# Layer 1's grouped experts: a counted loop written out tile by tile, with each tile's expert number loaded once and ahead

## The reference

```python
# layer 1, per token: gate over 9 experts, the two best, normalised
# expert e:  y = ( silu(x @ w1[e].T) * (x @ w3[e].T) ) @ w2[e].T
dim, hid, E, X = (128, 352, 8, 1)      # 8 + 1 experts, hidden width 352
TOP_K = 2
```

## Time and profile before

| | |
|---|---|
| median of 3 runs | 1991.06 us (1990.78 to 1992.78) |
| the profiled execution: its own time | 1985.47 us |
| its span, first to last instruction | 1983.8 us |
| PE busy over the span | 1555.5 us (78%), 12142 matmuls |
| DVE, ACT, POOL busy | 1341.1, 1044.5, 798.3 us |
| granted TensorE clock, mean | 0.905 of 2.4 GHz |

### The profile page before, as it was taken

One profiled execution on the slowest core, in us unless ns is written; L12 is line 12 of the kernel. 1 busy time (PEld: TensorE's weight loads), 2 busy tenths in 40 slices (PEclk: granted clock), 3 DMA queues, 4 the chain that ended last, 5 costly groups with the idle time before them and its releaser, 6 DMA issues. The chain is left out here.

```text
span 1983.8 us, 35609 instructions
## 1 busy us (share of the span) xinstructions
PE 1555.5 (78%) x12142; PEld 1065.2 (54%) x12143; DVE 1341.1 (68%) x2371; ACT 1044.5 (53%) x1857; POOL 798.3 (40%) x803
## 2 busy tenths in 40 slices
PE   5985887888865666636788889995489999869995
PEld 5753665665643444514566666663134444357884
DVE  7537777788799999585533337885873499556336
ACT  1458787787754545143433335663465477633441
POOL 1576555555698887257111113443320000006006
PEclk9997999999988888567899999997689999959998
DMA  4311111111000100456411113530652144021223
GB/s 146 99 62 52 52 38 46 51 34 46 17 26 25 31 23 10 161 186 159 70 44 44 42 44 68 89 62 20 175 88 51 33 67 66 5 90 54 87 79 85
DMA packets 153319, 130.35 MB, mean 66 GB/s; under 512 B 18929, under 2 KB 137864, under 8 KB 152914
## 3 DMA queue, kind: packets, MB, share of 16 engines
q1 hardware_dynamic: 140626, 104.57, 21.2%
q0 software_dynamic: 12544, 23.82, 4.6%
HBM read 77.08 MB, written 52.43 MB: 65 GB/s over the span
## 5 line engine op out<-in xcount | busy, mean ns | idle before, releaser
L667 POOL TENSOR_TENSOR xn_t<-xn_t,scan_du 128x512 f32<-128x512 f32 x256 | 321.6, 1270 | 179.9 <-ACT xn_t L809 100.0
L712 PE MATMUL banks<-scan_hc,ident 128*128 128x256 f32 x1024 | 294.9, 414 | 76.7 <-DVE scan_hc L864 76.7
L858 DVE TENSOR_TENSOR_SCAN xn_t<-banks,xn_t 128x512 f32<-128x512 f32 x256 | 311.3, 1216 | 42.0 <-ACT banks L799 35.7
L2287 ACT ACTIVATE att_pr<-banks 128x768 f32<-128x768 f32 (+1 forms) x256 | 234.2, 916 | 135.0 <-PE banks L2179 77.9
L799 ACT ACTIVATE banks<-delta,scan_exp_centre,a_neg 128x255 f32<-128x255 f32 x512 | 265.2, 559 | 49.9 <-DVE xn_t L858 49.4
L712 PEld LDWEIGHTS banks<-scan_hc,ident 128*128 128x128 f32 x1024 | 192.8, 207 | 139.6 <-DVE scan_hc L864 105.1
L864 DVE TENSOR_TENSOR scan_hc<-xn_t,banks 128x512 f32<-128x512 f32 x256 | 175.9, 687 | 26.8 <-PE banks L697 15.1
L918 POOL DMA_INDIRECT disp<-xn_tok,places x128 | 136.1, 1063 | 85.5 <-issue 61.3
L2332 DVE TENSOR_REDUCE att_mb<-banks 128x4 f32<-128x1024 f32 x128 | 153.9, 1221 | 22.9 <-PE banks L2146 18.1
L2195 PE MATMUL banks<-att_pr,att_vx 128*32 128x256 f32 (+1 forms) x2048 | 153.0, 372 | 5.0 <-ACT att_ot L2292 3.5
L2328 DVE TENSOR_REDUCE att_mb<-banks 128x6 f32<-128x768 f32 x128 | 121.5, 956 | 39.0 <-PE banks L2153 37.0
(11 more groups left out here) (360 smaller groups left out, 3340.0 us busy)
## 6 DMA issues: line engine op xcount, KB each, us to landing
scan_ew<-f_packed SPq DMA_DIRECT2D x12, 578.0 KB, 4.1
q_parts<-att_p_parts SPq DMA_DIRECT2D x16, 384.0 KB, 3.9
k_parts<-att_p_parts SPq DMA_DIRECT2D x16, 384.0 KB, 5.9
att_qs<-q_parts SPq DMA_DIRECT2D x64, 96.0 KB
att_ks<-k_parts SPq DMA_DIRECT2D x64, 96.0 KB
gau_ew<-f_packed SPq DMA_DIRECT2D x8, 578.0 KB
disp<-zeros SPq DMA_DIRECT2D x1, 4608.0 KB, 15.9
att_xin<-disp SPq DMA_DIRECT2D x72, 64.0 KB, 1.8
```

The source lines that it names most:

```text
L667: nc.gpsimd.tensor_tensor(bu[:, i % RING], b_sb[:, q % 2], du[:, b % 2, c:c + 1, :].to_broadcast([P, 2, T]), ALU.mult).then_inc(s.bu_made, 1)
L712: ins = nc.tensor.matmul(bank(Y_BANK)[:, c, :], g.ident[:], hc[:, i % RING, n, :], start=False, stop=(i % (PAIRS * DC) == PAIRS * DC - 1 a ...
L858: v.tensor_tensor_scan(rows(h[:, i % 2]), g.ps[:, DA + i % RING, :], rows(bu[:, i % RING]), 0.0, ALU.mult, ALU.add).then_inc(s.scan_done, 1)
L2287: nc.scalar.activation(pr[:, i % RING], g.ps[:, at:at + 2, 0:W], ACT.Exp, scale=scale).then_inc(s.p_ready, 1)
```

## The change

In `grouped`, the loop is gone: each engine's code is a Python `for` over all 72 tiles, so that every tile has instructions of its own, with DMA addresses and semaphore values as constants. Waits on values that are always reached are left out (first tiles), and so are the `sem_inc` that biased the counters. The order of the work on each engine is as before. On PE the expert number is loaded once a tile, into a register that `up` and, a tile later, `down` both use; the load stands behind `up(j+1)`, two tiles ahead. The matmuls still take the weights' address from a register.

```diff
-    def each(eng, body):
-        body(0, 0, 0, 0, 2)
-        body(1, 0, 1, 1, 2)
-        with eng.Fori(1, NJ // 2 - 1) as it:
-            for p in range(2):
-                body(it * 2 + p, it, p, 2, 2)
-        body(NJ - 2, NJ // 2 - 1, 0, 2, 1)
-        body(NJ - 1, NJ // 2 - 1, 1, 2, 0)
...
     def sync(sp):
         sp.wait_ge(r.scattered, 2 * NT * 16)
+        for j in range(NJ):
+            if j >= 2:
+                sp.wait_ge(s.turned, j - 1)
+            sp.dma_start(xin[:, j % 2, :], disp[j * P:(j + 1) * P, :]).then_inc(x_in[j % 2], 16)
...
-        def tile_expert(j):
-            return pe.value_load(r.tile_e[0:1, bass.ds(j, 1)], min_val=0, max_val=E1 - 1)
+        expert = {}
+        def load_expert(j):
+            if j < NJ:
+                expert[j] = pe.value_load(r.tile_e[0:1, j:j + 1], min_val=0, max_val=E1 - 1)
...
-        def up(j, p):
-            e = tile_expert(j)
+        def up(j):
             pe.wait_ge(s.xt_ready, j + 1)
...
-                                       rows(w13[:, bass.ds(e, 1), m * H1:(m + 1) * H1]), start=True, stop=True)
+                                       rows(w13[:, bass.ds(expert[j], 1), m * H1:(m + 1) * H1]), start=True, stop=True)
...
-        def down(j, p):
-            e = tile_expert(j)
...
+        load_expert(0)
+        load_expert(1)
+        transpose(0)
+        transpose(1)
+        up(0)
+        for j in range(NJ):
+            up(j + 1)
+            load_expert(j + 2)
+            transpose(j + 2)
+            turn_hidden(j)
+            down(j - 1)
+        down(NJ - 1)
```

More of the change, by code:

```diff
@@ L1223, in down @@
+        def down(j):
+            if j < 0:
+                return
+            p = j % 2
+            pe.wait_ge(s.ht_ready, j + 1)
+            if j >= 2:
+                pe.wait_ge(s.y_out, j - 1)
             for c, (lo, n) in enumerate(H1_CUTS):
                 ins = nc.tensor.matmul(g.ps[:, 4 * p, P:2 * P], ht[0:n, p, c, :],
-                                       rows(w2[0:n, bass.ds(e, 1), c * D:(c + 1) * D]),
-                                       start=(c == 0), stop=(c == len(H1_CUTS) - 1))
+                                       rows(w2[0:n, bass.ds(expert[j], 1), c * D:(c + 1) * D]),
+                                       start=(c == 0), stop=(c == NH - 1))
@@ L1227, in down @@
             ins.then_inc(s.y_ready, 1)
[L1229 to L1241, removed]
@@ L1252, in scalar, with silu @@
+        down(NJ - 1)
+        pe.wait_ge(s.y_out, NJ)
     def scalar(act):
         nc.scalar.preload_act_table(ACT.Silu)
-        act.sem_inc(s.ht_ready, 2)
-        def silu(j, p):
+        def silu(j):
+            if j >= NJ:
+                return
             act.wait_ge(s.ab_ready, j + 1)
[L1258 to L1263, removed]
+            if j >= 2:
+                act.wait_ge(s.h_ready, j - 1)
+            nc.scalar.activation(a[:, j % 2, :], g.ps[:, 4 * (j % 2) + 1, 0:H1], ACT.Silu).then_inc(s.a_ready, 1)
@@ L1264, in body @@
+        silu(0)
+        for j in range(NJ):
+            silu(j + 1)
             act.wait_ge(s.ht_turned, j + 1)
-            if before >= 2:
+            if j >= 2:
                 act.wait_ge(s.y_ready, j - 1)
-            n = H1_CUTS[-1][1]
+            p, n = j % 2, H1_CUTS[-1][1]
             nc.scalar.copy(ht[:, p, 0:2, :], g.ps[:, 4 * p + 3, 0:2 * P].rearrange("p (c t) -> p c t", c=2))
             nc.scalar.copy(ht[0:n, p, 2, :], g.ps[0:n, 4 * p + 3, 2 * P:3 * P]).then_inc(s.ht_ready, 1)
-        silu(0, 0)
@@ L1271, in scalar, with take @@
-        each(act, body)
     def vector(dve):
[L1274 to L1281, removed]
+        def take(j):
+            if j >= NJ:
+                return
+            dve.wait_ge(s.turned, j + 1)
+            nc.vector.tensor_copy(xt[:, j % 2, :], g.ps[:, 4 * (j % 2), 0:P]).then_inc(s.xt_ready, 1)
@@ L1289, in give @@
+        def give(j):
+            if j < 0:
+                return
+            p = j % 2
             dve.wait_ge(s.y_ready, j + 1)
-            if not isinstance(turn, int) or turn:
-                dve.wait_ge(stored[p], turn * 16)
+            if j >= 2:
+                dve.wait_ge(stored[p], j // 2 * 16)
             nc.vector.tensor_copy(yo[:, p, :], g.ps[:, 4 * p, P:2 * P]).then_inc(s.y_out, 1)
[L1294 to L1306, removed]
+        take(0)
+        take(1)
+        gated(0)
+        for j in range(NJ):
+            give(j - 2)
+            take(j + 2)
+            gated(j + 1)
+        give(NJ - 2)
+        give(NJ - 1)
     def gpsimd(pool):
-        def body(j, it, p, before, after):
-            pool.wait_ge(s.y_out, j + 3)
-            pool.dma_start(ybuf[bass.ds(j * P, P), :], yo[:, p, :]).then_inc(stored[p], 16)
@@ L1312, in gpsimd @@
-        each(pool, body)
+        for j in range(NJ):
+            pool.wait_ge(s.y_out, j + 1)
+            pool.dma_start(ybuf[j * P:(j + 1) * P, :], yo[:, j % 2, :]).then_inc(stored[j % 2], 16)
         for p in range(2):
-            pool.wait_ge(stored[p], NJ // 2 * 16)
+            pool.wait_ge(stored[p], len(range(p, NJ, 2)) * 16)
     job = Names()
```

53 lines of the change are left out of this document (28 added, 25 removed).

## The result

The changed kernel takes 1937.4 us (median of 4 runs, 1930.81 to 1939.94), the kernel before 1990.92 (4 runs beside them, 1989.99 to 1992.78). The ratio is 0.9732, with a 95% interval from 0.9713 to 0.975: 53.5 us faster. The forecast was 1940.5.

The account below looks back on a forecast made before the run. PE was taken to bound the stage, idle ahead of `up` while its sequencer loads a register and branches. Gains of 49.6 + 0.7 + 0.3 = 50.6 us from the 1991.06 us median gave 1940.5 us, range 1937 to 1957.

Parts of the forecast that it names:

- the two bounds: PE's period a tile without gaps: 2.29 us (gain 49.6 us) or 2.39 us (gain 42.8 us), from 3.02.
- the 0.10 us of the first matmul of `up`: First of `up`'s four matmuls takes 558 ns against 459; taken as the price of the pause before it.
- The margins of the moved load: Load between `up` and next transpose costs nothing: 0.3 us to spare at `xt`, 0.37 us at the transpose.
- Rival 1: A new wait at `xt` or the transpose takes part of the gain: 1961 us, or 1986 in full; chance 0.15.
- the second margin: Room at the transpose behind the moved load: 0.37 us, or about 0.2 if the load ends 0.3 us later.
- the wait at 1084.8: PE sequencer's wait ahead of `up`; its 51 ns, same as at L1235, read as not waiting for anything.
- The same load costs nothing elsewhere: Load ahead of `down` called free, since the sequencer was about 0.9 us ahead of its engine there.
- Hidden before, so worth nothing by itself: Removing each tile's second load, ahead of `down`, gains nothing itself but pays for the moved load.
- rival 2: Written-out code must be fetched, some 11 packets for PE: slower, 2001 us at 5.5 us a packet; chance 0.03.
- rivals 3 and 4: Denser PE granted a lower clock: 1958 us, chance 0.04; time given back behind the stage: 1990 us, chance 0.03.
- The head and the tail: Stage start: 0.3 us from loading the first expert number during PE's wait; last `up` and `down` gaps: 0.7 us.
- the sum: Whole gain: 49.6 us from tiles, 0.7 at the end, 0.3 at the head, 50.6 us; 1940.5 us from the median.

Follow-up runs that it names:

- e3: Changed kernel with a second register load and check right behind the first, its value unused: 2.451 us a tile, stage 189.5 us, median 2131.86 us.
- e10: Kernel before, with a third load, check and address a tile behind `up`, ahead of the transpose: 3.684 us a tile, ratio 1.0151 to 1.0238.
- e8: Changed kernel with its one load a tile moved to just ahead of `up`: 2.300 us a tile, stage 179.2 us, median 2110.59 us.
- e1: Changed kernel's straight code, but two loads a tile at their old places, ahead of `up` and `down`: 2.612 us a tile, stage 201.0 us, median 2142.76 us.
- e2: Loop kept, four tiles a turn on PE, one early load a tile into four registers, no bounds check: 2.293 us a tile, median 2126.34 us.
- e9: Kernel before without the bounds check of each load, loop and load places kept: 2.758 us a tile, stage 211.6 us, ratio 0.9841 to 0.9922.
- e11: Changed kernel with all SP input loads first and the attention's twelve loads held until after the stage: stage 171.6 us, median 2109.55 us.
- e4: Changed kernel unedited, run again on another chip: 2.292 us a tile, stage 179.2 us, median 2122.04 us, ratio 0.9747 to 0.9789.

## Why the prediction was right, point by point

**The bound, and the period of a tile.** Right. PE without gaps takes 2.292 us a tile, and of the two bounds 2.29 was the true one: the 0.10 us of the first matmul of `up` was the pause's. 68 x (3.019 - 2.292) is 49.4 where 49.6 was forecast.

**The margins of the moved load.** Right. `xt` was to be there 1.78 us behind `up`'s start, and the copy ends at 1.78 (1062.52 and 0.29, less 1061.03). The load lies beside `up`'s matmuls and PE waits for nothing. Rival 1 didn't occur. It isn't far off, though: a second load costs 0.16 us a tile (e3). Two steps of the working were unsound without harm. With a load 0.3 us longer the second margin would have been 0.07 us (3.47 - 3.4), not about 0.2. And the 51 ns of the wait at 1084.8 don't show that nothing was waited for: the row of L1210 above has 51 ns too, with half a microsecond of standing still behind it. What shows it is that the rows leave no gap: the check is over at 1084.65 and the instruction behind the wait starts at 1084.9.

**"The same load costs nothing elsewhere", and "Hidden before, so worth nothing by itself".** Wrong, and this is the step of the prediction that failed. I saw the sequencer 0.9 us ahead of its engine at the load ahead of `down` and took this lead for free time. But the sequencer of the kernel before never waited (no gap over 0.12 us). It had 3.02 us of instructions a tile against 2.29 us of PE's work. A lead that it had at one place was used up at the next, and a load at the hidden place made the next `up` later by as much: 0.665 us (e10). So the load ahead of `down` counted like the one ahead of `up`. In code written out it is enough that one of the two goes, whether the other stands ahead of `up` (e8: 2.300) or behind it (the changed kernel: 2.292). With the loop kept, no run takes away one load and nothing else. The gain came out right all the same, because it was computed from PE's floor and not from the loads: whatever brings the sequencer under 2.29 us gives 49 us, and what goes beyond gives nothing. That is luck as far as the reason goes: by the prediction an edit that only takes away the load ahead of `down` would have been costed at nothing, and from e1 to e8 that edit gave 21.7 us.

The runs put numbers on this budget. They have to be taken where the sequencer doesn't wait: 3.02 us in the kernel before, 2.45 in e3. So the loop's own instructions are 0.57 us a tile. Two loads of 0.665 us leave 2.45 - 1.33 = 1.12 us for all the rest of a tile in code written out, and with one load it needs 1.12 + 0.665 = 1.79 of 2.29 us. The 0.5 us left over is the half microsecond for which the changed kernel's sequencer is seen to stand still. e1 has the instructions of e3 and takes 0.16 us more: its loads stand behind the wait for `yo`, not ahead of it, and it waits there. So the place isn't always worth nothing. It can add a wait on top of the sum.

**The straight code is fetched; slower (rival 2).** Didn't occur, and neither did rivals 3 and 4. The granted clock is 1.00 in the stage, and the attention starts as much earlier as the stage is shorter. The page of the profile counts 100 instruction packets for the whole execution, where it counted 90 before (11 more were estimated), and PE has no idle time at all in the 100 us of the stretch.

**The head and the tail.** Both small. The 0.3 us of the first load came (from SP's issue to the first `up` 6.36 us instead of 6.65), but the first eight matmuls of `up` took 5.06 us instead of 4.34, and the head as a whole, the first step with it, lost 0.5 us. The tail gave 1.1 instead of 0.7. Together 49.4 - 0.5 + 1.1 is 50.0, as measured, where the sum had 50.6.

**The whole.** The range was 1937 to 1957, and 1937.4 lies at its lower edge, 3 us under the sum. The working had 2 us between runs, and the range went 3.5 us below the sum. The changed kernel's own runs spread over 9 us, which was the term I had made too small, and that the median still fell inside by 0.4 us is luck.

## What to carry to other kernels

Where PE's idle time is put down to an engine that had long been done, look whether its sequencer's rows follow one another without a gap, and add up what it does in a period: if that exceeds PE's work, each instruction costs its full length even where the sequencer is ahead, and the time falls until the sum is under PE's floor, and no further. So count register loads first (0.66 us each with the check), take away the easiest, and don't take a local lead of the sequencer for free room. The loop itself may stay where the sum allows it, as in e2. A wait for data can still come on top (e1, e9). To test whether a cost is hidden, double it.

## What was not expected of the hardware

- A register load with its check costs 0.665 us in sequence (e10), though its instruction lasts only 301 ns. The Trainium skill, "DMA: Bandwidth & Descriptors", section "Latency and other measured facts", gives such a load a floor of about 600 ns. The load itself is under that in every row here, 0.30 us at the median and 0.50 at the longest; the load with its check is near it.
- Short instructions take more room than their rows say. The loop left out was worth 0.57 us a tile to the sequencer (before less e3), while its branch, the longest instruction of it, lasts 0.208 us once in two tiles. The Trainium skill, "Perfetto Trace Analysis", section "Sequencer-only Instruction (DRAIN, etc)", says that the profile shows only the execution of such an instruction and leaves out the wait and the passing on of semaphores around it. The rows here agree: the wait at L1210 lasts 51 ns at 1062.3, the same as L1235 in the earlier trace rows, and the instruction behind it starts only at 1062.9, when the data is there.
- The matmuls at the head of the stage are slow even after a pause of 2.33 us: the first eight of `up` take 4.25 us (e11), where eight at full speed take about 2 x 1.45. The granted clock there is 1.00 from 1079.0 to 1083.4 us, with the pause in it and PE back at work since 1081.68, then 0.50 (1.2 GHz) to 1086.8, and 1.00 again. So the lower clock there isn't the 9 us wait's alone. What sets it stays open.
- The chips differ by 9% in the kernel before and in the changed one, and the changed one's stage differs by 0.4 us at most. In another chip's profile of the changed kernel (e4), between 90 and 155 us, ScalarE and VectorE stood in waits that don't occur on the first chip:

```profile
DVE delta L486 <- remote: 66.6, 2, 59.7
...
ACT front_gate L438 <- remote: 49.2, 1, 49.2
```

What they wait for is not known. Only ratios on one chip, and times within the stage, can be compared between the chips.
